# One seed tile for two stencil steps, and seven additions per half moved to VectorE, in a fused image block

## The reference, cut to what matters

```
h = h0 = fsrc = s0                      # s0: the normalized input
g, g1 = relu(bn(dwconv(h))), relu(bn(dwconv1(h)))
D, c0, E, cm_x, cp_x, cm_y, cp_y = ...  # pointwise from g, g1 and sobel(h), computed once
for _ in range(5):
    prev = h
    h = D * (c0*h0 - 2*E*h + cm_x*roll(h, 1, 2) + cp_x*roll(h, -1, 2)
                           + cm_y*roll(h, 1, 3) + cp_y*roll(h, -1, 3))
    h = h + D * (2*DT) * fsrc
    h0 = prev
```

## Time and profile before

| | us |
|---|---|
| median of 3 runs | 944.87 (944.26 to 946.18) |
| the profiled execution | 944.92 |
| its span, first to last instruction | 942.9 |
| PE busy | 769.6 (82%) |
| DVE busy | 796.8 (85%) |
| ACT busy | 549.7 (58%) |
| POOL busy | 512.8 (54%) |

### The profile page before, as it was taken

The page is one execution under the profiler, slowest core; times in us unless marked ns, Lnnn a source line. Parts: engine busy times, 40 slices in busy tenths (PEclk is TensorE's granted clock), DMA queues, the critical chain, the costliest instruction groups (busy, mean ns, idle before and its releaser), DMA issues. The chain is left out here.

```text
span 942.9 us, 10709 instructions
## 1 busy us (share of the span) xinstructions
PE 769.6 (82%) x3950; PEld 509.9 (54%) x3950; DVE 796.8 (85%) x671; ACT 549.7 (58%) x953; POOL 512.8 (54%) x240
## 2 busy tenths in 40 slices
PE   3999998987677678688799899898775677877895
PEld 2444443444376668578655444344445666766873
DVE  6899886269899998999989978724889999999983
ACT  3664232125849898979477433211484887897932
POOL 2005996020469697778410299901126979867841
PEclk9999999999889999999899999989998999999998
DMA  3000000000534455345200200000033455545421
GB/s 109 1 0 0 0 0 1 0 1 0 154 125 170 144 187 190 124 170 186 61 1 0 67 1 0 0 0 1 0 98 95 154 177 179 196 142 178 159 89 22
DMA packets 33296, 75.03 MB, mean 80 GB/s; under 512 B 15708, under 2 KB 15844, under 8 KB 33248
## 3 DMA queue, kind: packets, MB, share of 16 engines
q1 hardware_dynamic: 31840, 73.09, 23.1%
q0 software_dynamic: 320, 1.05, 0.5%
q10 hardware_dynamic: 1088, 0.26, 0.1%
HBM read 70.71 MB, written 2.62 MB: 78 GB/s over the span
## 5 line engine op out<-in xcount | busy, mean ns | idle before, releaser
L373 POOL TENSOR_TENSOR arena<-arena 128x1024 f32<-128x1024 f32 x85 | 202.0, 2387 | 48.3 <-DVE arena L1708 45.4
L934 ACT ACTIVATE arena<-arena 128x128 f32<-128x128 f32 (+3 forms) x408 | 152.5, 448 | 91.9 <-DVE arena L1635 75.3
L1708 DVE TENSOR_TENSOR_SCAN arena<-arena,ps 128x1024 f32<-128x1024 f32 x86 | 194.9, 2278 | 10.0 <-ACT arena L934 7.4
L934 ACT ACTIVATE arena<-arena,Amat 128x1024 f32<-128x1024 f32 x128 | 143.7, 1141 | 8.8 <-DVE arena L1708 7.5
L621 PE MATMUL ps<-mat,arena 128*128 128x128 f32 x1016 | 134.6, 276 | 3.9 <-POOL arena L373 3.4
L580 PE MATMUL ps<-mat,arena 128*128 128x128 f32 x560 | 77.1, 282 | 71.5 <-DVE arena L1708 35.3
L934 ACT ACTIVATE arena<-ps 128x1024 f32<-128x1024 f32 (+2 forms) x65 | 56.0, 873 | 114.1 <-PE ps L452 50.4
L621 PEld LDWEIGHTS ps<-mat,arena 128*128 128x128 f32 x1016 | 116.7, 143 | 7.2 <-POOL arena L373 5.3
L373 POOL TENSOR_TENSOR arena<-HS,arena 128x1024 f32<-128x1024 f32 x42 | 99.5, 2368 | 36.8 <-DVE HS L1708 34.7
L580 PEld LDWEIGHTS ps<-mat,arena 128*128 128x128 f32 x560 | 61.2, 139 | 89.1 <-DVE arena L1708 45.6
L740 PE MATMUL ps<-arena,mat 128*128 128x512 f32 x240 | 106.3, 592 | 0.0
(11 more groups left out here) (207 smaller groups left out, 1390.8 us busy)
## 6 DMA issues: line engine op xcount, KB each, us to landing
arena<-c_rows SPq DMA_DIRECT2D x128, 512.0 KB, 3.7
out<-arena SPq DMA_DIRECT2D x28, 64.0 KB, 2.5
xres<-x POOLq DMA_DIRECT2D x4, 256.0 KB, 5.4
xres<-x SPq DMA_DIRECT2D x4, 256.0 KB, 4.1
arena<-arena SPq DMA_DIRECT2D x4, 252.0 KB
convw<-conv_w SPq DMA_DIRECT2D x1, 576.0 KB
c_rows<-ROWS SPq DMA_DIRECT2D x4, 128.0 KB, 1.9
mat<-mats SPq DMA_DIRECT2D x1, 448.0 KB, 3.6
```

Of the source, the lines that this page charges most:

```text
L373: tt(HC[s % 2], HS[s % 3], CB[s % 4], ALU.mult).then_inc(S("hc"), 1)
L934: return nc.scalar.activation(out_, in_, func, bias=bias, scale=scale, accum_out=accum_out)
L1708: nc.vector.tensor_tensor_scan(HS[s % 3], DA[s % 3], PS[q][:, :], 0.0, ALU.mult, ALU.add).then_inc(S("scan"), 1)
```

## The change

In the first two steps the seed copied into PSUM is a new tile (kept in `g`) that holds source and h0 term in one; GpSimd makes it from a factor that ScalarE puts into `Y`. VectorE's first `previous` of each tile and TensorE's `g` matmuls of steps 0 and 1 go. Of the later steps, TensorE adds `g` in (0, 2), (1, 2), (0, 3) and (0, 4); for (1, 3) and (1, 4) VectorE adds it to its third product. GpSimd sums `R` and `XY` only where k equals t mod 2; in (1, 0), (0, 1), (1, 2), (0, 3) and (1, 4) VectorE does, right before `new_h`. The loops are written out.

```diff
+        def pool_adds(k, t):
+            return k == t % 2
+        def previous_on_pe(k, t):
+            return t in (2, 3) and (k, t) != (1, 3) or (k, t) == (0, 4)
...
-            def previous_product(h, k):
+            def first_source(h, k):
...
-                tt(img(a["g"]), img(a["P0"]), frm(a["fz"])[:, 1:33, 1:33], ALU.mult).then_inc(S(f"a{k}_g"), 1)
+                tt(img(a["g"]), img(a["Y"]), frm(a["fz"])[:, 1:33, 1:33], ALU.mult).then_inc(S(f"a{k}_g"), 1)
+
+            def row_neighbours(h, k, t):
...
+                tt(img(a["R"]), img(a["Pmx"]), hw[:, :, 0:32], ALU.mult)
+                tt(img(a["XY"]), img(a["G"]), hw[:, :, 2:34], ALU.mult).then_inc(S(f"a{k}_x"), 1)
+                if pool_adds(k, t):
+                    pool.wait_ge(S(f"a{k}_x"), 2 * it + 1)
+                    tt(a["G1"][:, :], a["R"], a["XY"], ALU.add).then_inc(S(f"a{k}_x"), 1)
...
+                first_source(h, 0)
                 source(h, 0)
-                previous_product(h, 0)
-                previous_product(h, 1)
+                first_source(h, 1)
...
+            def stencil_sum(h, k, t):                                  # TensorE
+                pe.wait_ge(S(f"a{k}_act"), 3 * it + 3)
+                if previous_on_pe(k, t):
+                    pe.wait_ge(S(f"a{k}_g"), 4 * h + t)
...
-                ins = av(a["P0"], a["Dc"], ACT.Identity, 2.0, -1.0)
...
+                av(a["P0"], a["Dc"], ACT.Identity, 2.0, -1.0)
+                if k == 0:
+                    av(a["Sc"], a["Dc"], ACT.Identity, 2 * DT)
+                act.wait_ge(S("a_K"), 2 * h + k + 1)
+                av(a["Y"][:, 0:L], a["Dc"], ACT.Identity, 2.0 + 2 * DT, -1.0).then_inc(S("a_P0"), 1)
...
+            def seed(h, k, t):
+                if t == 0:
+                    act.wait_ge(S(f"a{k}_g"), 4 * h + 1)
+                if t == 2:
+                    act.wait_ge(S("a_Sc1" if k else "a_Sc"), h + 1)
+                av(PS[2 * k][:, :], A[k]["g" if t < 2 else "Sc"], ACT.Identity).then_inc(S(f"a{k}_act"), 1)
...
             def products(h, k, t):
...
-                dve.wait_ge(S(f"mix{k}"), ONE + 2 * it)
...
+                if t < 2 or previous_on_pe(k, t):
+                    tt(img(a["X"]), img(a["Pe"]), field, ALU.mult).then_inc(S(f"a{k}_e"), 1)
+                else:
+                    tt(img(a["X"]), img(a["Pe"]), field, ALU.mult).then_inc(S("a_newton"), 1)
+                    dve.wait_ge(S("a_newton"), sums_before(h, k, t) + 1)
+                    dve.wait_ge(S(f"a{k}_g"), 4 * h + t)
+                    tt(a["X"][:, 0:L], a["X"][:, 0:L], a["g"], ALU.add).then_inc(S(f"a{k}_e"), 1)
...
             def new_h(h, k, t):
...
+                if not pool_adds(k, t):
+                    dve.wait_ge(S(f"a{k}_x"), 2 * it + 1)
+                    tt(a["G1"], a["R"], a["XY"], ALU.add).then_inc(S(f"a{k}_x"), 1)
+                dve.wait_ge(S(f"mix{k}"), mix_done(h, k, t))
+                dve.wait_ge(S(f"a{k}_x"), 2 * it + 2)
                 tt(wrapped(a["hw"])[:, :, 1:33], img(PS[2 * k]), img(a["G1"]), ALU.add).then_inc(S(f"a{k}_h"), 1)
...
-                with dve.Fori(0, STEPS - 2) as t:
-                    step(h, t)
-                    previous(h, 0, t + 1)
+                for t in range(STEPS - 1):
+                    new_h(h, 0, t)
+                    if t > 0:
+                        previous(h, 1, t)
+                    products(h, 0, t + 1)
+                    new_h(h, 1, t)
+                    if t < STEPS - 2:
+                        previous(h, 0, t + 1)
                     products(h, 1, t + 1)
-                step(h, STEPS - 2)
-                products(h, 1, STEPS - 1)
                 new_h(h, 0, STEPS - 1)
```

More of the change, by code:

```diff
@@ L209, in taps_done, with mix_taken, mix_done @@
             return sum(off_pe(*t) - 1 for t in tiles)
+        def pool_adds(k, t):
+            return k == t % 2
+        def previous_on_pe(k, t):
+            return t in (2, 3) and (k, t) != (1, 3) or (k, t) == (0, 4)
+        def mix_taken(h, k, t):
+            return mix_done(h, k, t) - 1
+        def mix_done(h, k, t):
+            return sum(1 + previous_on_pe(k, u) for u in range(STEPS)) * h + sum(1 + previous_on_pe(k, u) for u in range(t + 1))
         def conv_ps(h, k, w):
@@ L395, in _ @@
                     root(D[1], h - 1, 3, 1)
+                first_source(h, 0)
                 source(h, 0)
-                previous_product(h, 0)
-                previous_product(h, 1)
-                with pool.Fori(0, STEPS) as t:
+                first_source(h, 1)
+                for t in range(STEPS):
                     for k in range(2):
[L401 to L409, removed]
+                        row_neighbours(h, k, t)
                 for k in range(2):
@@ L529, in rolls @@
                 roll_up(h, k)
+            def stencil_sum(h, k, t):
+                a, it, mix = A[k], STEPS * h + t, PS[2 * k]
+                pe.wait_ge(S(f"a{k}_act"), 3 * it + 3)
+                if previous_on_pe(k, t):
+                    pe.wait_ge(S(f"a{k}_g"), 4 * h + t)
+                    for n in range(2):
+                        last = mm(half(mix, n), ident, half(a["g"], n), start=False, stop=False, skip_group_check=True)
+                    last.then_inc(S(f"mix{k}"), 1)
+                for name, count, mname, src in [("c", 2 * it + 1, "roll_up", "Pmy"), ("c", 2 * it + 2, "roll_down", "sden"),
+                                                ("e", it + 1, "ident", "X")]:
+                    pe.wait_ge(S(f"a{k}_{name}"), count)
+                    for n in range(2):
+                        last = mm(half(mix, n), mt(mname), half(a[src], n), start=False, stop=(name == "e"), skip_group_check=True)
+                last.then_inc(S(f"mix{k}"), 1)
             def conv_part(k, n, chosen):
@@ L724, in _ @@
                 rolls(h, 1)
-                with pe.Fori(0, STEPS) as t:
+                for t in range(STEPS):
                     for k in range(2):
[L727 to L741, removed]
+                        stencil_sum(h, k, t)
                 group_mean(D[0], h, 1, 0)
@@ L1252, in _ @@
                         act.wait_ge(S("a_Pe"), 2 * h + 1)
-                        seed(h, 0)
+                        seed(h, 0, 0)
                         from_D(h, 1)
@@ L1263, in _ @@
                     act.wait_ge(S("a_Q6"), 2 * h + k + 1)
-                    seed(h, k)
-                with act.Fori(1, STEPS) as t:
+                    seed(h, k, 0)
+                for t in range(1, STEPS):
                     for k in range(2):
@@ L1268, in _ @@
                         field(k)
-                        seed(h, k)
+                        seed(h, k, t)
                 for k in range(2):
@@ L1612, in minus_E, with products @@
                 tt(a["Pe"], a["Dc"], PS[2 * k][:, :], ALU.mult).then_inc(S("a_Pe"), 1)
-            def products(h, k, t, first=False):
+            def products(h, k, t):
                 a, it = A[k], STEPS * h + t
@@ L1617, in products @@
                 dve.wait_ge(S(f"a{k}_act"), 3 * it + 2)
-                dve.wait_ge(S(f"mix{k}"), ONE + 2 * it)
-                if first and h > 0 and k == 1:
+                if t == 0 and h > 0 and k == 1:
                     dve.wait_ge(S("stored1"), 128 * h)
@@ L1623, in products, with sums_before @@
                 dve.wait_ge(S("a_Pe"), 2 * h + k + 1)
-                tt(img(a["X"]), img(a["Pe"]), field, ALU.mult).then_inc(S(f"a{k}_e"), 1)
+                if t < 2 or previous_on_pe(k, t):
[5 more added lines that the diff above has]
+                    tt(a["X"][:, 0:L], a["X"][:, 0:L], a["g"], ALU.add).then_inc(S(f"a{k}_e"), 1)
+            def sums_before(h, k, t):
+                on_dve = [(b, u) for u in range(2, STEPS) for b in range(2) if not previous_on_pe(b, u)]
+                return 6 * h + 4 + on_dve.index((k, t))
             def previous(h, k, t):
                 a, it = A[k], STEPS * h + t
-                dve.wait_ge(S(f"mix{k}"), ONE + 2 * it + 1)
+                if t == 1:
+                    dve.wait_ge(S(f"a{k}_act"), 3 * it + 3)
+                elif previous_on_pe(k, t):
+                    dve.wait_ge(S(f"mix{k}"), mix_taken(h, k, t))
                 tt(img(a["g"]), img(a["P0"]), img(PS[2 * k + 1]), ALU.mult).then_inc(S(f"a{k}_g"), 1)
             def new_h(h, k, t):
-                a = A[k]
-                dve.wait_ge(S(f"mix{k}"), ONE + 2 * (STEPS * h + t + 1))
-                dve.wait_ge(S(f"a{k}_x"), 2 * (STEPS * h + t + 1))
-                tt(wrapped(a["hw"])[:, :, 1:33], img(PS[2 * k]), img(a["G1"]), ALU.add).then_inc(S(f"a{k}_h"), 1)
[L1637 to L1641, removed]
+                a, it = A[k], STEPS * h + t
+                if not pool_adds(k, t):
[3 more added lines that the diff above has]
+                dve.wait_ge(S(f"a{k}_x"), 2 * it + 2)
+                tt(wrapped(a["hw"])[:, :, 1:33], img(PS[2 * k]), img(a["G1"]), ALU.add).then_inc(S(f"a{k}_h"), 1)
             def add_stage0(h, k):
@@ L1773, in _ @@
```

(3 more changed lines are left out.)

22 lines of the change are left out of this document (8 added, 14 removed).

## The result

The changed kernel takes 954.7 us (four runs, 951.9 to 956.3) against 944.6; the ratio is 1.0105, 95% interval 1.0071 to 1.0138. The prediction was 952.7 with a range of 947.5 to 957.5. The profiled execution, with a span of 954.5 us (942.9 before), is the slowest of the four (956.3); a second one, taken for the first experiment, has 951.6.

A forecast was written before the change was run, and what follows sets the result against it. VectorE was to set the pace after the change: 62.6 us plus 3.2 of waits, 65.8 per stencil. That gave +2.8 us in the first half and +5.0 in the second, 944.9 + 7.8 = 952.7 us, range 947.5 to 957.5.

The forecast's parts named there:

- VectorE becomes the bound, one hand-over and three products to a sub-step: Stencil: a VectorE sub-step without additions takes 2.62 + 3 x 1.133 = 6.02 us, with or without `previous`.
- the 2.62 us floor: Stencil: a field's products can't start until ScalarE has copied it, 2.62 us after new_h starts.
- An addition costs 1.27 us: Stencil: each VectorE addition adds 1.27 us to its sub-step, including the wait for VectorE's own result.
- The waits of the additions: Stencil: additions reading two SBUF tiles are held off by GpSimd, 3.2 us a half in all.
- The first new_h: Stencil start: new_h(0, 0) comes 1.2 us earlier in the first half, nothing gained in the second.
- What I cost at nothing: Terms left out of the sum: ScalarE's Y, seed wait, g pairs and mix waits, written-out loops, TensorE's clock.
- The loops: Loops written out on the engines: taken as 0, bounds -1 and +2 us.
- TensorE has its result by then: Ahead of the second half's stencil: minus_E has TensorE's result with about 0.5 us to spare, despite Y's delay.
- TensorE's granted clock after its idle time in the stencil: More idle time in the stencil could bring a half-speed clock, covered in part: 0 to +2 us.
- No collision: Rival, stencil: additions run beside GpSimd without the 3.2 us of waits, 946.3 us; chance 0.08.
- The bare sum of VectorE's operations: Rival, stencil: VectorE's pace is the sum of its operations alone, 936.1 us; chance 0.06 for this or better.
- More collisions: Rival, stencil: each of six additions waits half a GpSimd product, 6.3 instead of 3.2 us, 959 us; chance 0.08.

The follow-up runs named there:

- the first experiment: The changed kernel, unaltered, timed again against the kernel before on another chip: 954.3 us, ratio 1.0108.
- its experiment: The changed kernel with its seven additions a half reading the field in PSUM instead of XY or g: 948.8 us, ratio 1.0040 to the kernel before.
- the mixed version: Changed kernel, but TensorE adds R of (1, 0) and all g of steps 2 to 4, VectorE sums only (0, 3), GpSimd the other eight: 936.9 us, ratio 0.9915.

## Why the prediction was right

*VectorE becomes the bound, one hand-over and three products to a sub-step.* Right to the hundredth: 6.02 us without an addition (116.40 to 122.42 in the first half), and removing `previous` altogether changed nothing, so the 2.62 us floor, the three products and the additions set it, and not the plain count of VectorE's operations.

*An addition costs 1.27 us.* Right within 0.04: 7.33 - 6.02 = 1.31 for the one at 128.43, and 62.69 for the whole stencil without meetings (62.6). With no meeting at all the stencils are still 1.6 us slower than before, so the additions' own time alone used up all that TensorE and GpSimd had been relieved of.

*The waits of the additions.* Laid out: 0.25, 0.2, 0, 2.2, 0.55, 0. Measured, as duration over 1.22 in the first half: 0.23, 0.12, 0, 2.15 (137.04), 0.57 (152.65), 0. The total by experiment is 3.1 us a half against 3.2. The durations are regular enough to lay out by hand. The meeting at 135.9 was decided by 0.07 us, which no schedule by hand resolves; the prediction had both orders at the same 2.2 us, so its sum does not hang on that. (No run shows the other order.)

*The first new_h.* 1.2 us earlier in the first half was laid out. Measured against x_neighbours of tile 1 (83.33 before, 84.05 after), that is with the 0.72 us taken off by which all of VectorE's work was late from 43 us on, it is 95.83 - (95.35 - 0.72) = 1.2. The second profile of the changed kernel has the same distance (82.49 to 93.78, 11.29 us, against 12.50 before). In the second half nothing, as laid out.

*What I cost at nothing.* The loops: right. Y: half right. The prediction had half a microsecond to spare for TensorE's result, and where the clock stayed at 2.4 GHz that held; the profile after shows VectorE idle there after all, 0.63 and 0.39 us:

```profile
534.54 1.23 DVE L1614 TENSOR_TENSOR arena<-arena 128x1024 f32<-128x1024 f32 x1 [0.63 <-PE ps L714]
...
541.83 1.22 DVE L1628 TENSOR_TENSOR arena<-arena,ps 128x1024 f32<-128x1024 f32 x1 [0.39 <-PE ps L529]
```

The step that failed is "TensorE has its result by then": I had moved TensorE's work by Y's delay at the full clock, and it then ran part of it at half. That is 1.0 us of the 2.3 by which the forecast, 7.8 over before, stays under the 10.0 and 10.1 measured. Against it stands that Y in the kernel before did not move the median; its interval allows at most 0.6 us more.

The other term put at nothing is TensorE's granted clock after its idle time in the stencil (bounds 0 to +2). The idle time came as laid out, 1.67 us ahead of (1, 1) and 4.11 ahead of (0, 4). Behind the latter the g pair, 1.88 us elsewhere, ran at half speed:

```profile
144.09 3.78 PE L553 MATMUL ps<-arena,mat 128*128 128x512 f32 x4 [4.11 <-ACT ps L950]
```

Inside the stencil this is covered, since no new_h waits for TensorE. Behind the stencil it is not. The first 18 matmuls of the convolution, before and after:

```profile
161.51 9.69 PE L463 MATMUL ps<-arena,convw 128*128 128x512 f32 x18 [3.81 <-ACT arena L934]
```

```profile
165.03 10.77 PE L479 MATMUL ps<-arena,convw 128*128 128x512 f32 x18 [4.69 <-ACT arena L950]
```

Both start 3.89 us after the last new_h, but TensorE has been idle 4.69 us instead of 3.81, its granted clock over the 10 us from the last new_h is 0.66 instead of 0.83, and they take 1.1 us longer. In the second half they take 10.98 us instead of 10.44; in the second profile of the changed kernel 10.09 and 10.95. So 0.9 to 1.6 us of the changed kernel's time stand here, within the bounds but not in the sum, and about what is missing. No experiment takes this term out by itself, so it is read from profiles and not shown as the cause. The stretches outside the stencils also differ by 3 us between two profiles of one and the same kernel (820.0 and 823.0 us for the changed one), along with the places where TensorE's granted clock fell.

Two numbers of the prediction are not right as they stand, and nothing else hangs on them. The second half runs 455.6 us later (550.22 - 94.6), not 55.6. And the range 947.5 to 957.5 is narrower than the bounds of the waits from which it is said to be made: 0 to 6.3 us a half give 946.3 to 959.

*The rivals.* No collision was 946.3 us: its experiment gave 948.8, with the stencils at 62.7, which is the number of that rival with 2.5 us on it that lie outside them. That run takes the meetings away; in the changed kernel itself they are there, so the rival is out. The bare sum of VectorE's operations fell with the kernel without `previous`. More collisions did not come: the waits were the ones laid out.

## What to carry to other kernels

When work is moved off a full engine, count what the taker has in a period with its hand-overs: here VectorE showed 2 us idle in 14, room for one or two operations, but a floor of 6.02 us per sub-step (the wait for ScalarE's copy and three products) left only 0.7 to 0.85 us under the pace of before, and every addition takes 1.27. An addition of two SBUF tiles on VectorE beside a busy GpSimd costs its own time and up to one GpSimd operation more; TensorE, adding a tile through the identity into a sum that it builds anyway, met nobody in these runs (the mixed version's stencils are within 0.1 us of the schedule). And change the shares one by one: of this change the common seed was worth 2.8 us, the seed with five sums on VectorE 3.5 (the two intervals overlap), and the two additions of g turned that into a loss of 10.

## What the runs showed of the hardware

- Where two operations of VectorE and GpSimd that read only SBUF met, the one issued first went on and the other stood still, down to 0.07 us: the addition issued at 135.89 took 1.23 us, the GpSimd sum issued at 135.96 took 3.36 instead of 2.36. With one operand in PSUM the same additions took 1.21 to 1.22 us throughout.
- The Trainium skill (SBUF — State Buffer, "Who interferes with whom") states that a VectorE instruction with at most one SBUF input, outside the modes that take both ports, does not contend with GpSimd. That holds here: 1.22 against 3.37 us.
- 0.7 us more of TensorE's idle time at one place went with the lower granted clock (1.2 GHz) in the group behind it (3.5 to 3.65 us instead of 2.05), in nine of ten profiles, and in none of the four without that idle time. The piece of the kernel around it took 29.7 to 29.8 us instead of 28.7 to 28.8. A delay that fits into the slack at full clock may not fit at half.
